# Source-term rows and the first seven maxima of a dense attention made in the stage before it, their masks loaded ahead of most edge counts

## The reference, cut to what matters

```
hp = h @ W2.T
e  = hp[src] . a_src + hp[dst] . a_dst ;  e = leaky_relu(e, 0.2)
e_max = segment_max(e, dst) ;  ex = exp(e - e_max[dst])
alpha = ex / (segment_sum(ex, dst) + 1e-16)
out = segment_sum(hp[src] * alpha, dst)          # added to x
```

## Time and profile before

| | us |
|---|---|
| median of three runs | 4440.61 (4436.75 to 4441.31) |
| the profiled execution | 4433.63 |
| its span | 4431.5 |
| stage of the features | about 1605.2 to 1634.8 |
| dense attention | about 1634.8 to 1997 |

### The profile page before, as it was taken

How to read it: one execution, slowest core, us unless ns; L and a number is a source line. 1 busy time by engine, 2 the same in 40 slices (tenths; PEclk the granted TensorE clock), 3 DMA queues, 4 the chain that set the end, 5 groups by cost and what they waited for, 6 DMA issues and landing times. The chain is left out here.

```text
span 4431.5 us, 67081 instructions
## 1 busy us (share of the span) xinstructions
PE 3562.0 (80%) x23854; PEld 3125.8 (71%) x23854; DVE 2733.1 (62%) x6790; ACT 1643.8 (37%) x4314; POOL 1259.0 (28%) x1266
## 2 busy tenths in 40 slices
PE   4777774854777777998999999799999699959696
PEld 3566663643656566784888888689999599949695
DVE  6899986554888848864777777742234433353444
ACT  1345451212444444552666666521110122320131
POOL 6777751726777710000000000000000122200263
PEclk8788886976888888999999999999998799979798
DMA  5455542244555563500000000043444311153324
GB/s 157 133 159 144 159 117 99 94 108 122 145 158 143 158 164 94 148 1 15 1 1 1 1 1 1 21 122 112 121 121 150 115 37 37 36 135 107 136 71 129
DMA packets 196534, 418.05 MB, mean 94 GB/s; under 512 B 54821, under 2 KB 127659, under 8 KB 195840
## 3 DMA queue, kind: packets, MB, share of 16 engines
q1 hardware_dynamic: 135296, 250.07, 19.8%
q0 software_dynamic: 60928, 164.04, 13.2%
HBM read 329.61 MB, written 84.35 MB: 93 GB/s over the span
## 5 line engine op out<-in xcount | busy, mean ns | idle before, releaser
L825 POOL DMA_INDIRECT sb<-features,sb x850 | 836.2, 984 | 262.1 <-issue 257.8
L1965 PE MATMUL ps<-sb 128*128 128x125 f32 x5400 | 688.4, 283 | 73.9 <-DVE sb L2024 73.1
L1965 PEld LDWEIGHTS ps<-sb 128*128 128x128 f32 x5400 | 636.4, 191 | 125.9 <-DVE sb L2024 115.2
L2255 PE MATMUL ps<-sb 125*125 125x256 f16 x5000 | 570.0, 275 | 15.8 <-DVE sb L2355 15.8
L2255 PEld LDWEIGHTS ps<-sb 125*125 125x125 f16 x5000 | 557.4, 138 | 21.1 <-issue 16.0
L136 POOL IOTA sb<- 128x56 f32 (+9 forms) x30 | 5.5, 218 | 1668.5 <-POOLq L105 1585.6
L1991 ACT ACTIVATE sb<-ps 128x125 f32<-128x125 f32 x1350 | 360.6, 276 | 254.9 <-PE ps L1965 254.9
L2960 ACT ACTIVATE sb<-ps,sb 128x128 f32<-128x128 f32 x784 | 221.0, 376 | 546.6 <-PE ps L2888 545.2
L1122 PE MATMUL ps<-sb 128*125 128x260 f32 x1700 | 385.3, 385 | 9.8 <-PEq L1120 9.3
L2888 PE MATMUL ps<-sb 128*128 128x128 f32 x3136 | 382.6, 277 | 1.8 <-DVE sb L2929 1.8
L1122 PEld LDWEIGHTS ps<-sb 128*125 128x125 f32 x1700 | 318.0, 189 | 91.3 <-issue 40.1
(11 more groups left out here) (323 smaller groups left out, 5251.0 us busy)
## 6 DMA issues: line engine op xcount, KB each, us to landing
sb<-adj SPq DMA_DIRECT2D x125, 683.6 KB
neg<-sb SPq DMA_DIRECT2D x25, 683.6 KB
adj<-sb SPq DMA_DIRECT2D x25, 683.6 KB
sb<-neg SPq DMA_DIRECT2D x25, 683.6 KB
sb<-rows_y SPq DMA_DIRECT2D x30, 560.0 KB
sb<-in_L_ffn_W SPq DMA_DIRECT2D x16, 1024.0 KB
sb<-features,sb POOLq DMA_INDIRECT x850
sb<-adj SPq DMA_DIRECT2D x125, 79.3 KB
```

The costliest lines, as they stand in the source:

```text
L825: e.indirect_dma_start(hgs[i % 4][:, w, :], None, k.HR, indirect(ids[i % 3][:, w:w + 1])).then_inc(*hg_in[i % 4].by(16))
L1965: return e.matmul(k.PS[:, b, 0:NC], V[:, y, row, :], self.old_h(n)[:, y, :], start=False, stop=y == 1, skip_group_check=True)
L2255: m = e.matmul(self.k.PS[0:P, v % 2, 0:D], self.ads[v % self.RING][:, j * P:j * P + P], part[:, j, :], start=j == 0 and x == 0, stop=j == ...
```

## The change

A class `Ahead` owns SR, the maxima M, the ring of mask buffers and its semaphores over both stages. In the stage of the features TensorE, after the term columns and before the head products, makes the source rows from XT: seven groups, each with two matmuls of up to 500 columns whose stationary operand is the term column of the weights, broadcast. ScalarE copies them to SR, and VectorE makes maxima 0 to 6 before it copies the terms into SD. The second pair of head products waits until the source rows are read. SyncE loads masks 0 to 2, the counts of blocks 0 to 3, masks 3 to 6 (each after its buffer's release), and then counts 4 to 12. In the attention the rows made on the identity are now only those of R1, mask loads begin with 7, and the terms of set 0 follow at once. The early counts have one semaphore for each set.

```diff
@@ -709,10 +709,12 @@
     def banks(self, i):
         return (6 + 2 * i) % 8
 
-    def tensor(self, e):
+    def tensor(self, e, ahead=None):
         k = self.k
         e.wait_ge(*self.w_in.at(16))
         for i, ts in enumerate(PAIRS):
+            if ahead and i == 1:
+                e.wait_ge(*ahead.read.at(7))
             if i < 4:
                 self.turned.wait(e, 3 + i)
             else:
@@ -1246,39 +1248,97 @@
     def __init__(self, k, ctx):
         self.k, self.flat = k, k.sb(ctx, [P, 13 * N + 1], f16)
         self.ADS = self.flat[:, 0:13 * N].rearrange("p (n c) -> p n c", c=N)
-        self.early, k.early.count = k.early, 0
-
-    def load(self, e, x, sig):
+        self.early = k.early
+        for s in self.early:
+            s.count = 0
+
+    def load(self, e, x, sig, some=range(7)):
         for n, t in enumerate(SETS[x]):
-            two_starts(e, self.ADS[:, self.SLOTS[x] + n, :], self.k.ADJ16[t], sig)
+            if n in some:
+                two_starts(e, self.ADS[:, self.SLOTS[x] + n, :], self.k.ADJ16[t], sig)
 
     def of(self, x, j):
         return self.ADS[:, self.SLOTS[x]:self.SLOTS[x] + len(SETS[x]), j * P:j * P + P]
 
-    def sync(self, e):
-        for x in range(2):
-            self.load(e, x, self.early)
-
-
-def dense_attention(k, counts, HA, SD, H1):
-
+    def sync(self, e, ahead):
+        if ahead:
+            ahead.masks(e, range(0, 3))
+        self.load(e, 0, self.early[0], range(0, 4))
+        if ahead:
+            ahead.masks(e, SETS[0][3:])
+        self.load(e, 0, self.early[0], range(4, 7))
+        self.load(e, 1, self.early[1])
+
+
+class Ahead:
+
+
+
+
+    def __init__(self, k, ctx, H1):
+        flat = H1[:, :, :].rearrange("p t d -> p (t d)")
+        self.k, self.SR, self.R1, self.M = k, flat[:, 0:N], flat[:, N:2 * N], k.sb(ctx, [P, T])
+        self.negs = [k.sb(ctx, [P, N], bf16) for _ in range(3)]
+        self.neg_in, self.neg_used = k.neg_in, k.neg_used
+        for s in (*k.neg_in, k.neg_used):
+            s.count = 0
+
+    def signals(self, k):
+        self.full, self.read = k.sig("source_full"), k.sig("source_read")
+
+    def masks(self, e, bs):
+        for b in bs:
+            if b >= 3:
+                e.wait_ge(*self.neg_used.at(b - 2))
+            two_starts(e, self.negs[b % 3][:, :], self.k.NEG[b], self.neg_in[b % 3])
+
+    def tensor(self, e, heads):
+
+        heads.turned.wait(e, 6)
+        for g, ts in enumerate(GROUPS):
+            if g == 6:
+                e.wait_ge(*self.read.at(1))
+            n = len(ts) * P
+            for h in range(2):
+                m = e.matmul(self.k.bank(g % 6, n, P), heads.w[:, h, D:D + 1].broadcast_to([128, P]),
+                             heads.turned.XT[:, h, ts[0] * P:ts[0] * P + n], start=h == 0, stop=h == 1)
+            m.then_inc(*self.full.by())
+
+    def scalar(self, e):
+        for g, ts in enumerate(GROUPS):
+            n = len(ts) * P
+            e.wait_ge(*self.full.at(g + 1))
+            e.activation(self.SR[:, ts[0] * P:ts[0] * P + n], self.k.bank(g % 6, n, P),
+                         ACT.Copy).then_inc(*self.read.by())
+
+    def vector(self, e):
+        e.wait_ge(*self.read.at(7))
+        for b in SETS[0]:
+            self.maximum(e, b)
+
+    def maximum(self, e, b):
+        e.wait_ge(*self.neg_in[b % 3].at(32 * (b // 3 + 1)))
+        e.tensor_tensor_reduce(out=self.negs[b % 3][:, :], in0=self.SR, in1=self.negs[b % 3][:, :], scale=1.0,
+                               scalar=-HUGE, op0=ALU.subtract, op1=ALU.max,
+                               accum_out=self.M[:, b:b + 1]).then_inc(*self.neg_used.by())
+
+
+def dense_attention(k, counts, ahead, HA, SD):
 
 
 
     nc = k.nc
     with ExitStack() as ctx:
-        M, c1, c2, s2, s8, sc = (k.sb(ctx, [P, T]) for _ in range(6))
+        M, neg_used = ahead.M, ahead.neg_used
+        c1, c2, s2, s8 = (k.sb(ctx, [P, T]) for _ in range(4))
         s, d = SD[:, :, 0], SD[:, :, 1]
-        flat = H1[:, :, :].rearrange("p t d -> p (t d)")
-        SR, R1 = flat[:, 0:N], flat[:, N:2 * N]
+        R1 = ahead.R1
         R2 = [k.sb(ctx, [P, 7 * P]) for _ in range(2)]
-        negs = [k.sb(ctx, [P, N], bf16) for _ in range(3)]
         work = [k.sb(ctx, [P, 7 * P]) for _ in range(7)]
         rec = k.sb(ctx, [P, 7])
         units = [(x, j) for x in range(4) for j in range(T)]
-        rows = [(v, g) for v in range(2) for g in GROUPS]
         halves = [(x, ts) for x in range(4) for ts in (SETS[x][0:4], SETS[x][4:])]
-        ads_in, neg_in, neg_used = k.sigs("ads_in", 2), k.sigs("neg_in", 3), k.sig("neg_used")
+        ads_in = k.sigs("ads_in", 2)
         vs, terms_set, max_set = k.sig("vstep"), k.sig("terms_set"), k.sig("max_set")
         rows_full, rows_read, half_full, half_read = (
             k.sig(x) for x in ("rows_full", "rows_read", "half_full", "half_read"))
@@ -1291,19 +1351,13 @@
         with k.block() as block:
             @block.sync
             def _(e):
-                def load_masks(bs):
-                    for b in bs:
-                        if b >= 3:
-                            e.wait_ge(*neg_used.at(b - 2))
-                        two_starts(e, negs[b % 3][:, :], k.NEG[b], neg_in[b % 3])
-
-                load_masks(range(0, 16))
+                ahead.masks(e, range(7, 16))
                 e.wait_ge(*masked.at(T))
                 counts.load(e, 2, ads_in[0])
-                load_masks(range(16, 22))
+                ahead.masks(e, range(16, 22))
                 e.wait_ge(*masked.at(2 * T))
                 counts.load(e, 3, ads_in[1])
-                load_masks(range(22, T))
+                ahead.masks(e, range(22, T))
 
             @block.tensor
             def _(e):
...
@@ -1311,9 +1365,7 @@
                     x, ts = halves[q]
                     if q % 2 == 0:
                         e.wait_ge(*max_set.at(x + 1))
-                    if q == 0:
-                        e.wait_ge(*rows_read.at(8))
-                    else:
+                    if q > 0:
                         e.wait_ge(*half_read.at(q))
                     for n, t in enumerate(ts):
                         m = e.matmul(k.PS[0:P, 7, n * P:n * P + P], c2[:, t:t + 1].broadcast_to([P, P]),
@@ -1321,16 +1373,14 @@
                     m.then_inc(*half_full.by())
 
                 e.wait_ge(*terms_set.at(1))
-                for n, (v, ts) in enumerate(rows):
-                    if n >= 8:
-                        e.wait_ge(*rows_read.at(n - 7))
+                for n, ts in enumerate(GROUPS):
                     for x, t in enumerate(ts):
-                        m = e.matmul(k.PS[0:P, n % 8, x * P:x * P + P], (sc, c1)[v][:, t:t + 1].broadcast_to([P, P]),
+                        m = e.matmul(k.PS[0:P, n, x * P:x * P + P], c1[:, t:t + 1].broadcast_to([P, P]),
                                      k.ident[0:P, 0:P], start=True, stop=True)
                     m.then_inc(*rows_full.by())
                 spread_half(0)
                 spread_half(1)
-                e.wait_ge(*rows_read.at(14))
+                e.wait_ge(*rows_read.at(7))
                 for u, (x, j) in enumerate(units):
                     if x < 3 and j == 15:
                         spread_half(2 * x + 2)
@@ -1352,11 +1402,11 @@
                     e.wait_ge(*half_full.at(q + 1))
                     e.activation(R2[x % 2][:, lo:lo + n], k.bank(7, n, P), ACT.Copy).then_inc(*half_read.by())
 
-                for n, (v, ts) in enumerate(rows):
+                for n, ts in enumerate(GROUPS):
                     e.wait_ge(*rows_full.at(n + 1))
                     lo, m = ts[0] * P, len(ts) * P
-                    e.activation((SR, R1)[v][:, lo:lo + m], k.bank(n % 8, m, P), ACT.Copy).then_inc(*rows_read.by())
-                e.wait_ge(*rows_read.at(14))
+                    e.activation(R1[:, lo:lo + m], k.bank(n, m, P), ACT.Copy).then_inc(*rows_read.by())
+                e.wait_ge(*rows_read.at(7))
                 for u in range(len(units) + 3):
                     if u < len(units):
                         x, j = units[u]
@@ -1381,12 +1431,6 @@
 
             @block.vector
             def _(e):
-                def maximum(b):
-                    e.wait_ge(*neg_in[b % 3].at(32 * (b // 3 + 1)))
-                    e.tensor_tensor_reduce(out=negs[b % 3][:, :], in0=SR, in1=negs[b % 3][:, :], scale=1.0,
-                                           scalar=-HUGE, op0=ALU.subtract, op1=ALU.max,
-                                           accum_out=M[:, b:b + 1]).then_inc(*neg_used.by())
-
                 def maxima_terms(x):
                     lo, hi = SETS[x][0], SETS[x][-1] + 1
                     m, c, dx = M[:, lo:hi], c2[:, lo:hi], SD[:, lo:hi, 1]
@@ -1409,13 +1453,9 @@
                         e.scalar_tensor_tensor(k.X[:, t, :], k.PS[0:P, i, 0:256], rec[:, i:i + 1], k.X[:, t, :],
                                                ALU.mult, ALU.add).then_inc(*sums_read.by())
 
-                e.tensor_copy(sc[:, :], s)
```

(41 more changed lines are left out.)

## The result

The changed kernel takes 4433.17 us, the median of 14 runs (4426.37 to 4438.59), against 4440.26 us for the kernel before in as many (4435.9 to 4444.38). The ratio is 0.9982, with an interval of [0.9975, 0.9989], which leaves out 1: 7.1 us faster, under 0.2%. Forecast were 7.6 us less and 4433.0 us. The profiled execution of the changed kernel took 4438.59 us, the longest of its 14 and 5 us longer than the profiled execution before, so I don't compare whole spans. (In one later set of runs, 1 of the 19 executions of the kernel before took 5501 us at a lower granted clock; it is left out, and the median of the other 18, 5005.84 us, is what those runs are compared with.) I compare positions counted from SyncE's first load in the features' stage, which is 1605.23 before and 1607.65 after.

The account below looks back on a forecast made before the run. TensorE sets the overall pace; before the attention the DMA queue binds, then VectorE. Mask 7 at 1681.4 instead of maximum 7 at 1688.99 gives 7.6 us off 4440.6: 4433.0 us, range 4425.5 to 4438.5.

Parts of the forecast that it names:

- TensorE's source rows: Features' stage, before the head products: seven groups of two matmuls add 10.7 us, hidden if VectorE is still later.
- Seven maxima in the features' stage: VectorE's maxima 0 to 6 run there, waiting for DMA between them, and end the stage at about 1652.5, 17 us later.
- The list of signs: What would show the forecast: among others, waits for DMA before maxima 3 to 6 and some 12 us before maximum 7.
- The hole in the queue at mask 6: Features' stage: mask 6, released only by maximum 3's end, leaves a DMA queue gap of 0.6 us, within 0 to 1.5.
- a drop of the share for more than 2 us near 1642: DMA share around mask 6's release: such a drop was named as a sign that the forecast is wrong.
- The tile at 3.25 us: DMA queue: each mask or counts tile of 0.78 MB takes 3.25 us, with bounds of 3.0 and 3.4.
- its 18 issues: Features' stage, SyncE: 18 issues of counts behind mask 6 take 8 to 12.5 us, done by 1651 to 1655.3.
- Mask 7 as the new wait: Head of the attention: mask 7, now tile 21, comes at 1681.4, 12 us after maximum 7 could start at 1669.
- Everything behind moves rigidly: Attention after its first matmul: TensorE sets the pace and the same steps release later loads, so the 7.6 us gain stays.
- The second rival: Attention start: the queue does not bind, sums ready at 1669 set the start; gain 20 us, 4421 us, chance 0.06.
- The third rival: No gain: mask 6's gap and slower tiles take it, or something else starts the attention; 4440 us, chance 0.05.
- the fourth: Features' stage: SyncE's wait for maximum 3 delays nine counts and mask 7; slower, loses from 7.6 us delay, chance 0.04.

Follow-up runs that it names:

- half-rows run: Changed kernel without the second of the two matmuls in each group of source rows: 4994.21 against 5002.17 us for the kernel before, 0.9982.

## Why the prediction held

The time was 4433.17 us for 4433.0 forecast. The mechanism held step by step; that the number came out within 0.2 us is luck, since the same kernel gained 7.1, 8.9 and 11.1 us in three sets of runs, and 6.8, 4.6 and 9.7 us at the start in three profiles.

- TensorE's source rows: 10.6 us measured for 10.7 us, hidden as said; the half-rows run shows it for half of them.
- Seven maxima in the features' stage, with VectorE ending it: maximum 0 at 17.8 for 17.7, the copy of the terms at 47.2 for 47.1. Mask 3 was waited for as said (33.8 for 33.4). The list of signs spoke of waits before maxima 3 to 6; only maximum 3 had one.
- The hole in the queue at mask 6: I took 0.6 us within 0 to 1.5. The windows show shares of 0.75, 0.18, 0.54 and 0.52 from 1643 to 1647, together 2.0 us short of a full queue: a term that was mis-sized by 1.4 us. The prediction had named a drop of the share for more than 2 us near 1642 as a sign that it is wrong. Taken by its words the sign came (1642 there is 1644.4 here, and three windows are near a half or under it), and the forecast held all the same, so it was drawn too tight: a hole costs what is missing from a full share, not its length. The tile at 3.25 us held in this profile (76.99 - 1.47 - 2.1 - 3.8 - 2.0 = 67.6 us for 21 tiles, 3.22), and its 0.6 us less for 21 tiles hid part of the hole. In the two other profiles mask 7 came 2.2 us later and 2.9 us sooner.
- SyncE: its 18 issues took 7.52 us, a little under the lower bound of 8, and ended at 1653.3, before VectorE.
- Mask 7 as the new wait: 12.69 us for 12, the start at 83.5 for 82.7. Moving it up the queue by two and six tiles moved the start by what the tiles are worth, so this cause is shown and not only argued.
- Everything behind moves rigidly: not quite. A single execution gave back 1.1 to 4.7 us of what was gained at the start, by the clock behind short waits and by how soon the mask behind the reloaded counts is there. The prediction had no term for either. The 14 runs show 7.1 us all the same, near the 6.8 at the start.
- What a measurement tells: the prediction put it at 8.9 us. With 14 runs of each the interval leaves out 1 at 7.1 us.

The second rival was the right upper end: without the wait for mask 7 it said 20 us, and the version with mask 7 moved up gained 21. The Trainium skill (DMA: Bandwidth & Descriptors, Bandwidth) has some 358 GB/s for HBM loads of a core. By that, an estimate, a tile takes 2.2 us and the wait would not exist in the changed kernel either. The trace does not agree: the full queue ran at 242 GB/s here. The third rival falls with the interval. The mechanism of the fourth, a late release of mask 6 that holds back all behind it, was at work, with a hole of 2.0 us where some 8 would have been needed to lose. The run with the masks last is slower for another reason: its first mask is as late as before, and the head comes behind the maxima.

## What to carry to other kernels

Where several kinds of tiles share one DMA queue, write down the queue as a list with one time per tile, and look up the place of each tile that something waits for, the one after the last that is moved too: here the seven masks went ahead, and the eighth, there at 1684.64, stayed behind six blocks that TensorE's matmuls of set 1 use only from 1748.60 on. Work moved to an earlier stage costs nothing while something else ends that stage. A part of a change can lose by itself and gain with the rest: the moved work lost 9.9 us under the old order and gained 7.1 with the new one. A wait of TensorE of 2.3 to 2.5 us in a stretch that it bounds can cost more than itself, by the lower clock that followed in about half of the cases.

## What the runs showed of the hardware

- The same 21 tiles in the same order took 74.1 (on another chip), 77.0 and 79.2 us from the stage's start in three executions of one kernel, 7% apart between the extremes, and the start of the attention moved with it (80.6, 83.5 and 85.7). Other work and the order were the same; what sets the pace of the queue in one execution stays open.
- A wait of TensorE of 2.3 to 2.5 us between long busy stretches was followed by a granted clock of 0.50 in about half of the cases (14 of 27), and no such fall came at the same place in the 12 cases without the wait. A longer stretch also followed some waits of 3.36 us (22.70 against 21.04 us for 96 matmuls). What decides stays open.
- A matmul of 500 f32 columns costs by its columns as one of 258 does, at a granted clock of 1.00: 10.6 us for 6250 columns, 1.69 ns each against 1.71, and its stationary operand can be one column, broadcast.
